# Turning a third of each head's softmax blocks by DMA instead of by TensorE in a fused decoder layer

## The chip, the cores and the metric

The kernel runs on one core of a Trainium2 chip. The metric is the device time of one execution in microseconds (us). Before the change it was 1101.77 us, the median of three runs (1101.6 to 1101.96).

## The reference, cut to what matters

The layer is attention, a residual and a LayerNorm, then a gated block that picks one of four experts by token, then a sparse feed-forward block. The change touches attention alone. There are 4 batches of 512 tokens, width 512, 16 heads of width 32, all in fp32:

```python
scores = jnp.einsum('bthd,bshd->bhts', q, k)
mask = jnp.tril(jnp.ones((T, T), dtype=scores.dtype))
scores = scores * mask                       # masked scores are 0, not minus infinity
attn = jax.nn.softmax(scores / T ** 0.5, axis=-1)
out = jnp.einsum('bhts,bshd->bthd', attn, v).reshape(B, T, H * Dh)
return out @ Wo
```

## The kernel before, in words

**Tiling.** Queries are cut into four rows of 128 (r = 0 to 3). Row r needs the keys of blocks 0 to r, which makes 1 + 2 + 3 + 4 = 10 blocks of 128 by 128 a head; what lies above the diagonal enters through sums. A head's rows are handled as three units (`row_blocks`, line 191): unit 0 is rows 2 and 0 (4 blocks), unit 1 is row 3 (4 blocks), unit 2 is row 1 (2 blocks). A batch has 16 heads, so 48 units, and there are 4 batches.

**One unit.** TensorE multiplies the scores into one of three PSUM banks `S` (`scores`). VectorE masks them and takes the maxima (`maxima`, `negated`). ScalarE takes the exponential into an SBUF tile `probs` (`exps`, signal `s_e`). TensorE turns each block with a transpose against `ident` into one of two PSUM banks `TP` (`transposes`, line 505, signal `s_T`). ScalarE copies the turned bank to fp16 (`hi`, line 697), VectorE subtracts that copy from the bank, which gives the low fp16 half (`lo`, line 870, signal `s_lo`). TensorE multiplies both halves by the values, two matmuls a block (`values`, line 521). Once a head's units are through, ScalarE copies the head out (`copy_out`, line 722), which sets `s_oe`.

**Order.** Each engine has one loop over the units, written out by hand. In iteration u TensorE does the transposes of unit u, the scores of unit u + 3, a piece of a projection (three matmuls over 512 columns, `pieces`), and the values of unit u - 2. ScalarE does the exponential of u, then `hi` of u - 1, then, in some iterations, the upper half of a projection (`split_at`) and the copy of a head. VectorE does the maxima of u + 2, `lo` of u - 1, then the split's lower half. GpSimd adds the parts of a head up. In batches 0 to 2 the projections of the rest of this batch and the first half of the next run beside the heads; in the last batch they end at unit 21. After the last unit of a batch stand the value projection of the next batch, the turn of the heads and the output product (`between`); in the last batch `finish`.

**SyncE.** Each projected group g of 128 columns of q or k goes out to DRAM in two DMAs of 256 KB (`halves_out`) and comes back in another arrangement in four of 256 KB (`stack_in`). SyncE runs through these as their inputs become ready, with the load of the next batch's turned x (1 MB, line 420), the load of x for the residual (1 MB, line 427) and, in the last batch, the context (4 MB) between them. All of them are issued from the one queue of SyncE.

Batches, iterations and units are numbered from 0, as in the code; batch 3 is the last.

Of the kernel before, what the change touches and what calls it, by code (L numbers as in the profile page):

```python
# [45 lines left out]
def attention(nc, w_dram, w_split, stacks, ident, idx_all, x_t, x_raw, s_xraw, x_rows,  # L46
# [17 lines left out]
    AHEAD_S, AHEAD_MAX, AHEAD_HI, AHEAD_LO, AHEAD_V = 3, 2, -1, -1, -2  # L64
    RP = 4
# [3 lines left out]
    with ExitStack() as ctx:  # L69
# [17 lines left out]
        probs = [sb(f"probs{i}", [P, T], F32) for i in range(RP)]  # L87
        pt_hi = [sb(f"pt_hi{i}", [P, T], F16) for i in range(RP)]
# [4 lines left out]
        ot_hl = [[sb(f"ot_{h}{i}", [P, KT, P], F32R) for i in range(2)] for h in ("hi", "lo")]  # L93
# [97 lines left out]
        row_blocks = ((2, 0), (3,), (1,))  # L191
# [3 lines left out]
        def places_of(rows):  # L195

            at = [sum((r + 1) * P for r in rows[:i]) for i in range(len(rows) + 1)]
            return list(zip(rows, at)), at[-1]

# [14 lines left out]
        G_AHEAD = 4  # L214
# [9 lines left out]
        turn_at = {25: 0, 33: 1, 46: 2}  # L224
# [164 lines left out]
        def _(sp):  # L389
# [21 lines left out]
            def stack_up(b, g):  # L411
                halves_out(b, g)
                stack_in(b, g)

            def batch(b, more):
                if more:

                    wait_apart(sp, s_passed_sp, [(s_xl, (b + 1) * KT)])
                    sp.wait_ge(s_z, PRIMED + b * NB)
                    sp.dma_start(x_turned, x_t[b + 1]).then_inc(s_xraw, 16)  # L420
                for g in range(G_AHEAD, 2 * NM):
                    stack_up(b, g)

                sp.wait_ge(s_xl, (b + 1 + more) * KT)
                if not more:
                    sp.wait_ge(s_z, PRIMED + b * NB)
                sp.dma_start(x_res, x_rows[b]).then_inc(s_xres, 16)
                if not more:

                    sp.wait_ge(s_pj, B * 2 * NM)  # L430
                    for e in range(len(context.raw)):
                        context.load(sp, e)
                if more:
                    for g in range(2 * NM, 2 * NM + G_AHEAD):
                        stack_up(b, g)
# [20 lines left out]
            for g in (2, 3):  # L456
                halves_out(0, g)
            for g in (2, 3):
                stack_in(0, g)
# [5 lines left out]
        def _(pe):  # L465
# [18 lines left out]
            def scores(b, u):  # L484
# [5 lines left out]
                if u >= SR:  # L490

                    pe.wait_ge(s_e, b * UPB + u - SR + 1)
# [1700 lines left out]
```

## Time and profile before

| | us |
|---|---|
| median of three runs | 1101.77 |
| the profiled execution | 1103.12 |
| its span, first to last instruction | 1101.4 |
| PE busy | 1040.3 (94%) |
| DVE busy | 738.3 (67%) |
| ACT busy | 486.6 (44%) |
| granted TensorE clock, mean | 0.989 |

PE is TensorE, PEld its weight loads, DVE VectorE, ACT ScalarE, POOL GpSimd, SP or SPq SyncE. The attention part ends at about 428 us of the span; what follows (experts, feed-forward) is TensorE work that the change does not touch. The shares above are means over both parts, so they say little of the loop over the heads. There, a timeline of one engine is the view to read. A line of it has the start in the span, the duration, the engine, the line of the kernel, the operation and its tiles. A record can last longer than the distance to the next one, because instructions overlap; where work is added up below, it is the distance from start to start that counts.

### The profile page before, as it was taken

Reading aid. Unit: us, or ns where it says so; the run is one execution under the profiler, and the core shown is the slowest. Engines: PE = TensorE matmul, PEld = TensorE weight load, DVE = VectorE, ACT = ScalarE, POOL = GpSimd, SP = SyncE. Lnnn points to the kernel's source line nnn. Section 1 sums busy time; section 2 is a strip of 40 time slices with the busy share of each in tenths; the row PEclk is TensorE's granted clock in tenths of the full one; section 3 lists DMA queues with packets and bytes.
Section 4 is the critical chain, followed back from the end, with each engine's and each line's share of the span. In section 5 each row is a group of like instructions: output and inputs, shape, how many; then the busy total and the mean of one; then the engine's idle time right before and its main releaser. Section 6 shows DMA issues by size and latency. Waiting matters only on the chain.

```text
span 1101.4 us, 18098 instructions
## 1 busy us (share of the span) xinstructions
PE 1040.3 (94%) x6022; PEld 840.1 (76%) x6023; DVE 738.3 (67%) x1768; ACT 486.6 (44%) x904; POOL 294.7 (27%) x496
## 2 busy tenths in 40 slices
PE   7889998999999875999999999999999999999995
PEld 6667776777777664788888888888888888888884
DVE  6798699778868886566657546445565545654766
ACT  5688488758857884222324222221232122222125
POOL 2186348545643641223220005100000000000224
PEclk9999999999999997999999999999999999999998
DMA  8877366727743742224532003310020001100112
GB/s 263 229 195 195 87 199 188 193 81 183 204 124 106 184 172 76 68 76 153 191 132 90 1 1 39 39 39 1 1 77 10 28 0 38 38 1 1 39 39 77
DMA packets 55217, 106.19 MB, mean 96 GB/s; under 512 B 6240, under 2 KB 8288, under 8 KB 55136
## 3 DMA queue, kind: packets, MB, share of 16 engines
q1 hardware_dynamic: 50256, 90.99, 29.9%
q0 software_dynamic: 4880, 14.18, 3.4%
q8 instruction: 44, 0.72, 0.3%
q14 instruction: 37, 0.30, 0.1%
HBM read 72.11 MB, written 30.94 MB: 94 GB/s over the span
## 4 chain that ended last, share of the span: by engine, by line
PE 58%; DVE 2%; ACT 1%; DMA 0%; issue 0%; POOLq 0%; POOL 0%; ACTq 0%; DVEq 0%
PE f_bank L42 55%; PE f_bank L1636 1%; PE f_bank L1644 1%; PE f_bank L1706 1%; PE f_bank L1660 0%; DVE beats L1973 0%; DVE h L1998 0%; DMA rows<-sorted_dram 0%; DVE rows_kept L2021 0%; ACT rows_kept L1067 0%; ACT fsg L1843 0%; DVE ln_stats L1039 0%; DVE rows_kept L2032 0%; ACT L1890 0%; POOLq L1410 0%
## 5 line engine op out<-in xcount | busy, mean ns | idle before, releaser
L1809 ACT ACTIVATE fsg<-f_bank 128x512 f32<-128x512 f32 x64 | 38.2, 597 | 299.7 <-PE f_bank L42 290.6
L1959 DVE TENSOR_TENSOR h<-f_bank,fsg 128x512 f32<-128x512 f32 x64 | 44.3, 692 | 181.3 <-PE f_bank L42 177.8
L687 ACT ACTIVATE probs<-bank,nmax 128x384 f32<-128x384 f32 (+3 forms) x256 | 131.7, 549 | 16.1 <-DVE nmax L861 13.2
L505 PE MATMUL bank<-ident,probs 128*128 128x128 f32 x640 | 108.6, 284 | 26.8 <-DVE pt_lo L870 13.3
L845 DVE CUSTOM_DVE_ANT_0 bank<-bank,mask 128x384 f32<-128x384 f32 (+3 forms) x256 | 123.3, 504 | 13.9 <-PE bank L494 12.7
L1072 POOL TENSOR_SCALAR ln_var<-ln_mv 128x1 f32<-128x1 f32 x39 | 9.0, 230 | 453.2 <-DVE ln_mv L1041 451.9
L870 DVE TENSOR_TENSOR pt_lo<-bank,pt_hi 128x512 f16<-128x512 f32 (+1 forms) x192 | 115.1, 599 | 16.9 <-ACT pt_hi L697 16.7
L697 ACT ACTIVATE pt_hi<-bank 128x512 f16<-128x512 f32 (+1 forms) x192 | 104.9, 547 | 28.2 <-PE bank L505 27.5
L42 PE MATMUL bank<-x_hi,w_qk 128*128 128x512 f32 x256 | 101.8, 415 | 6.1 <-DVE x_lo L875 5.8
L42 PE MATMUL f_bank<-wd_hi,hs_hi 128*128 128x512 f32 x256 | 99.9, 390 | 0.8 <-issue 0.8
L42 PE MATMUL f_bank<-wd_hi,hs_lo 128*128 128x512 f32 x256 | 99.8, 390 | 0.0
L42 PE MATMUL f_bank<-wd_lo,hs_hi 128*128 128x512 f32 x256 | 99.6, 389 | 0.0
L505 PEld LDWEIGHTS bank<-ident,probs 128*128 128x128 f32 x640 | 66.7, 140 | 39.0 <-ACT probs L687 23.7
L42 PE MATMUL f_bank<-big_hi,wg_hi 128*128 128x512 f32 x240 | 93.8, 391 | 0.0
L42 PE MATMUL f_bank<-big_lo,wg_hi 128*128 128x512 f32 x240 | 93.6, 390 | 0.0
L42 PE MATMUL f_bank<-big_hi,wu_lo 128*128 128x512 f32 x240 | 93.5, 390 | 0.0
L42 PE MATMUL f_bank<-big_hi,wg_lo 128*128 128x512 f32 x240 | 93.4, 389 | 0.0
L42 PE MATMUL f_bank<-big_hi,wu_hi 128*128 128x512 f32 x240 | 93.4, 389 | 0.0
L42 PE MATMUL f_bank<-big_lo,wu_hi 128*128 128x512 f32 x240 | 93.4, 389 | 0.0
L494 PE MATMUL bank<-big_lo 128*128 128x384 f32 (+3 forms) x256 | 83.0, 370 | 1.8 <-DMA big_lo<-k_lo_dram 1.8
L521 PEld LDWEIGHTS bank<-v,pt_hi 128*128 128x128 f16 x640 | 49.4, 97 | 37.8 <-issue 27.3
L1973 DVE TENSOR_TENSOR beats<-mag 128x512 bf16<-128x512 f32 (+4 forms) x51 | 56.2, 1158 | 30.6 <-ACT mag L1821 30.6
(262 smaller groups left out, 2470.4 us busy)
## 6 DMA issues: line engine op xcount, KB each, us to landing
big_lo<-q_hi_dram SPq DMA_DIRECT2D x32, 256.0 KB
big_lo<-q_lo_dram SPq DMA_DIRECT2D x32, 256.0 KB
big_lo<-k_hi_dram SPq DMA_DIRECT2D x32, 256.0 KB, 3.9
big_lo<-k_lo_dram SPq DMA_DIRECT2D x32, 256.0 KB, 5.2
rows<-sorted_dram SPq DMA_DIRECT2D x19, 256.0 KB, 2.7
q_hi_dram<-q_hi SPq DMA_DIRECT2D x16, 256.0 KB, 3.2
q_lo_dram<-q_lo SPq DMA_DIRECT2D x16, 256.0 KB, 3.1
k_hi_dram<-k_hi SPq DMA_DIRECT2D x16, 256.0 KB, 3.6
```

Source lines behind the costliest of these rows:

```text
L42: ins = pe.matmul(out, a(k, i), b(k, j), start=(n == 0), stop=(n == len(chain) - 1))
L494: ins = pe.matmul(S[u % SR][:, at:at + cols(r)], stack[0][m % 2][:, h, r * P:(r + 1) * P], stack[1][m % 2][:, h, 0:cols(r)], start=True, s ...
L505: ins = pe.transpose(TP[u % TR][:, j * P:(j + 1) * P], probs[u % RP][:, j * P:(j + 1) * P], ident[:, :])
L521: ins = pe.matmul(out[:, at:ONE + 1], p, v3[:, j, c, at:ONE + 1], start=(n == 0), stop=(n == len(chain) - 1))
L687: ins = act.activation(probs[u % RP][:, at:at + cols(r)], S[u % SR][:, at:at + cols(r)], ACT.Exp, bias=nmax[:, r, c:c + 1])
L697: act.activation(pt_hi[u % RP][:, 0:n], TP[u % TR][:, 0:n], ACT.Copy).then_inc(s_hi, 1)
L845: dve.tensor_tensor_reduce(out=S[u % SR][:, at:at + cols(r)], in0=S[u % SR][:, at:at + cols(r)], in1=mask[:, T - cols(r):T], scale=1.0, sc ...
L870: dve.tensor_tensor(pt_lo[u % RP][:, 0:n], TP[u % TR][:, 0:n], pt_hi[u % RP][:, 0:n], ALU.subtract).then_inc(s_lo, 1)
L1636: ins = pe.transpose(XB[q % 2][:, k * P:(k + 1) * P], rows[q][:, k * P:(k + 1) * P], ident[:, :])
L1809: act.activation(fsg[v % 2][:, :], GB[v % 2][:, :], ACT.Silu).then_inc(s_sg, 1)
L1959: dve.tensor_tensor(h[r % 2][:, j, :], UB[v % 2][:, :], fsg[v % 2][:, :], ALU.mult).then_inc(s_h, 1)
L1973: dve.tensor_tensor(beats[:, at:at + w, tw], mag[:, i:i + 1, tw].broadcast_to([P, w, tw.stop - tw.start]), mag[:, i + 1:J, tw], ALU.is_ge) ...
```

## The change

Units become rows 1 and 0 (3 blocks), row 2 (3 blocks), row 3 (4 blocks). The first of them is not turned by TensorE any more. Its exponential is written to the PSUM bank `TP` that its transposes would have filled (bank `S[0]` for unit 0 of a batch), ScalarE and VectorE split it there into the fp16 halves `p_hl` (128 x 768), and SyncE issues one transposing DMA from `p_hl` to `p_turned` (`turn`), six blocks of 128 by 128. There are two such pairs of tiles (`RD`). TensorE's values of that unit come last in its head (`valued`), and all values come three units behind instead of two (`AHEAD_V`). TensorE has no transposes in an iteration whose unit is turned by DMA.

The exponential of such a unit gets a wait on `s_lo` of the unit two before it, since it writes the bank that this one is read from. SyncE goes through the units in order: at each third unit it waits for `s_lo` and issues the turn; the transfers that it issued as they became ready are now tied to units (`in_at`, `out_at`, `X_AT`, `RES_AT`, `CTX_AT`), and the context comes in 16 pieces of 256 KB, one a unit from unit 27. The output halves `ot_hl` are placed over other tiles.

```diff
-    AHEAD_S, AHEAD_MAX, AHEAD_HI, AHEAD_LO, AHEAD_V = 3, 2, -1, -1, -2
-    RP = 4
+    AHEAD_S, AHEAD_MAX, AHEAD_HI, AHEAD_LO, AHEAD_V = 3, 2, -1, -1, -3
+    RP, RD = 4, 2
...
-        row_blocks = ((2, 0), (3,), (1,))
+        row_blocks = ((1, 0), (2,), (3,))
...
+        def by_dma(u):
+
+            return u % UPH == 0
...
+        def valued(slot):
+
+            return slot + 1 if slot % UPH < UPH - 1 else slot - (UPH - 1)
...
+        out_at = {0: 3, 6: 4, 12: 5, 18: 6, 21: 7, 33: 8, 36: 9, 45: 10}
+        in_at = {0: 2, 3: 3, 9: 4, 15: 5, 24: 6, 27: 7, 39: 8, 42: 9}
+        X_AT, RES_AT, CTX_AT = 0, 42, 27
...
+            def turn(b, u):
+
+                d = b * HEADS + u // UPH
+                n = places_of(units[u][2])[1]
+                wait_apart(sp, s_passed_sp, [(s_lo, b * UPB + u + 1)])
+                if d >= RD:
+                    sp.wait_ge(s_pv, b * UPB + slot_of(u) - RD * UPH + 1)
+                sp.dma_start(p_turned[d % RD][:, 0:2 * n // P, :], p_hl[d % RD][:, 0:2 * n],
+                             transpose=True).then_inc(s_pt[d % RD], 16)
...
             def batch(b, more):
+                for u in range(UPB):
+                    if by_dma(u):
+                        turn(b, u)
+                    if u in in_at and due(b, more, in_at[u]):
+                        stack_in(b, in_at[u])
+                    if u in out_at and due(b, more, out_at[u]):
+                        halves_out(b, out_at[u])
+                    if u == X_AT and more:
+
+                        wait_apart(sp, s_passed_sp, [(s_xl, (b + 1) * KT)])
+                        sp.wait_ge(s_z, PRIMED + b * NB)
+                        sp.dma_start(x_turned, x_t[b + 1]).then_inc(s_xraw, 16)
+                    if u == RES_AT:
+
+                        sp.wait_ge(s_xl, (b + 1 + more) * KT)
+                        if not more:
+                            sp.wait_ge(s_z, PRIMED + b * NB)
+                        sp.dma_start(x_res, x_rows[b]).then_inc(s_xres, 16)
+                    if not more and 0 <= u - CTX_AT < KT * len(context.raw):
+
+                        if u == CTX_AT:
+                            sp.wait_ge(s_pj, B * 2 * NM)
+                        context.load(sp, *divmod(u - CTX_AT, KT))
...
-            def values(b, u):
+            def values(b, slot):
+                u = valued(slot)
...
-                pe.wait_ge(s_lo, b * UPB + u + 1)
+                if by_dma(u):
+                    d = b * HEADS + c
+                    pe.wait_ge(s_pt[d % RD], 16 * (d // RD + 1))
+                else:
+                    pe.wait_ge(s_lo, b * UPB + u + 1)
...
-                    if u < UPB:
+                    if u < UPB and not by_dma(u):
                         transposes(b, u)
...
+                if by_dma(u):
+                    to = S[u % SR] if u == 0 else TP[u % TR]
+                    if u > 0:
+
+                        act.wait_ge(s_lo, b * UPB + u - TR + 1)
...
                 n = places_of(units[u][2])[1]
-                act.wait_ge(s_T, b * UPB + u + 1)
...
+                if by_dma(u):
+                    act.wait_ge(s_e, b * UPB + u + 1)
...
-                    if u % UPH == 2 and UPH <= u < UPB:
-                        copy_out(b, u // UPH - 1)
+                    if u % UPH == 0 and u >= 2 * UPH:
+                        copy_out(b, u // UPH - 2)
```

## Rows read from the trace of the kernel before

**Rows 1.** Loops, batches 1-3: PE, PEld, DVE, ACT, POOL busy; clock, DMA share, GB/s.
```profile
138.00:209.00 71.00, 65.17 (x608) 51.02 (x606) 66.03 (x255) 59.84 (x136) 45.87 (x75) 1.00 0.68 194
239.00:310.00 71.00, 65.79 (x611) 51.28 (x610) 61.72 (x224) 60.31 (x137) 42.10 (x71) 1.00 0.70 190
340.00:405.00 65.00, 55.12 (x569) 44.61 (x567) 58.08 (x219) 57.83 (x132) 36.61 (x67) 1.00 0.63 191
```

**Rows 2.** Timeline of PE in batch 1: start, duration, line, output and inputs, count.
```profile
201.16 0.41 PE L505 MATMUL bank<-ident,probs 128*128 128x128 f32 x2
201.33 0.36 PE L494 MATMUL bank<-big_lo 128*128 128x256 f32 x1
201.53 0.40 PE L42 MATMUL bank<-x_hi,w_qk 128*128 128x512 f32 x1
...
202.23 0.22 PE L521 MATMUL bank<-v,pt_hi 128*128 128x97 bf16 x1
...
202.63 0.66 PE L505 MATMUL bank<-ident,probs 128*128 128x128 f32 x4
203.05 0.48 PE L494 MATMUL bank<-big_lo 128*128 128x384 f32 x2
```

**Rows 3.** Timeline of ACT there; in brackets idle time before, and its releaser.
```profile
203.20 0.72 ACT L687 ACTIVATE probs<-bank,nmax 128x512 f32<-128x512 f32 x1
203.77 0.64 ACT L697 ACTIVATE pt_hi<-bank 128x512 f16<-128x512 f32 x1
204.25 0.52 ACT L687 ACTIVATE probs<-bank,nmax 128x256 f32<-128x256 f32 x1
204.67 0.60 ACT L697 ACTIVATE pt_hi<-bank 128x512 f16<-128x512 f32 x1
205.76 0.50 ACT L722 ACTIVATE o_part<-bank 128x388 f32<-128x388 f32 x1 [0.50 <-POOL rsum L247]
206.16 0.83 ACT L687 ACTIVATE probs<-bank,nmax 128x384 f32<-128x384 f32 x2
206.87 0.40 ACT L697 ACTIVATE pt_hi<-bank 128x256 f16<-128x256 f32 x1
207.13 0.71 ACT L687 ACTIVATE probs<-bank,nmax 128x512 f32<-128x512 f32 x1
...
210.07 0.49 ACT L722 ACTIVATE o_part<-bank 128x388 f32<-128x388 f32 x1 [0.27 <-PE bank L521]
```

**Rows 4.** The same in batch 3, past the last projection.
```profile
397.74 0.49 ACT L722 ACTIVATE o_part<-bank 128x388 f32<-128x388 f32 x1
...
401.64 0.49 ACT L722 ACTIVATE o_part<-bank 128x388 f32<-128x388 f32 x1
```

**Rows 5.** DVE line 870: its group at 512 columns, one instruction at 256.
```profile
L870 DVE TENSOR_TENSOR pt_lo<-bank,pt_hi 128x512 f16<-128x512 f32 x128 | 88.0, 687 | 4.9 <-ACT pt_hi L697 4.9
...
207.30 0.42 DVE L870 TENSOR_TENSOR pt_lo<-bank,pt_hi 128x256 f16<-128x256 f32 x1
```

**Rows 6.** Who waited for whom in the loop of batch 1: total, times, longest.
```profile
ACT pt_hi L697 <- PE bank L505: 7.4, 7, 4.0
PEld bank L505 <- ACT probs L687: 4.9, 12, 0.9
```

**Rows 7.** The page's DMA queue of SyncE: packets, MB, share of 16 engines.
```profile
q1 hardware_dynamic: 50256, 90.99, 29.9%
```

**Rows 8.** Landings of the 32 stores of line 397, 256 KB each.
```profile
DMA to landing us min/median/max: 2.0/3.5/5.3
```

**Rows 9.** SyncE's issues in batch 1, then the stretch in which they moved.
```profile
177.08 1.28 SPq L408 DMA_DIRECT2D big_lo<-k_hi_dram  x2
178.41 0.91 SPq L408 DMA_DIRECT2D big_lo<-k_lo_dram  x2
181.05 0.40 SPq L427 DMA_DIRECT2D x_raw<-x  x1
...
178.00:186.00 8.00, 7.26 (x70) 5.74 (x67) 6.74 (x28) 6.82 (x17) 7.11 (x10) 1.00 0.94 262
```

More of the change, by code:

```diff
@@ L87, in attention @@
         probs = [sb(f"probs{i}", [P, T], F32) for i in range(RP)]
+        with ExitStack() as octx:
+            ot_hl = [[octx.enter_context(nc.sbuf_tensor(f"ot_{h}{i}", [P, KT, P], F32R)) for i in range(2)]
+                     for h in ("hi", "lo")]
         pt_hi = [sb(f"pt_hi{i}", [P, T], F16) for i in range(RP)]
@@ L92, in attention @@
         o_tmp = [sb(f"o_tmp{i}", [P, NB - 1, HPT, HD], F32) for i in range(2)]
-        ot_hl = [[sb(f"ot_{h}{i}", [P, KT, P], F32R) for i in range(2)] for h in ("hi", "lo")]
+        p_hl = [sb(f"p_hl{i}", [P, 2 * WIDE * P], F16) for i in range(RD)]
+        p_turned = [sb(f"p_turned{i}", [P, 2 * WIDE, P], F16) for i in range(RD)]
+        s_pt = [sem(f"s_pt{i}") for i in range(RD)]
         mask = sb("mask", [P, T], F32)
@@ L409, in stack_in @@
                                  scratch[side][half].rearrange("(h r) t -> r h t", r=HD)).then_inc(s_st[side], 16)
-            def stack_up(b, g):
-                halves_out(b, g)
-                stack_in(b, g)
-            def batch(b, more):
-                if more:
[L418 to L435, printed above, removed]
+            def turn(b, u):
[6 more added lines that the diff above has]
+                             transpose=True).then_inc(s_pt[d % RD], 16)
@@ new lines, in due @@
+            def due(b, more, g):
+                return (more or g < 2 * NM) and (g >= G_AHEAD or b == 0)
+            def batch(b, more):
+                for u in range(UPB):
[18 more added lines that the diff above has]
+                        context.load(sp, *divmod(u - CTX_AT, KT))
+                if more:
+                    stack_in(b, 2 * NM + G_AHEAD - 2)
+                    halves_out(b, 2 * NM + G_AHEAD - 1)
+                    stack_in(b, 2 * NM + G_AHEAD - 1)
@@ L455, in _ @@
                 sp.dma_start(wo_raw[k], w_dram[3][:, k, :]).then_inc(s_wo_in, 16)
[L456 to L459, printed above, removed]
+            halves_out(0, 2)
             for b in range(B):
@@ L504, in transposes @@
                 for j in range(places_of(rows)[1] // P):
-                    ins = pe.transpose(TP[u % TR][:, j * P:(j + 1) * P], probs[u % RP][:, j * P:(j + 1) * P],
-                                       ident[:, :])
+                    ins = pe.transpose(TP[u % TR][:, j * P:(j + 1) * P],
+                                       probs[turned_index(u) % RP][:, j * P:(j + 1) * P], ident[:, :])
                 ins.then_inc(s_T, 1)
-            def values(b, u):
+            def values(b, slot):
+                u = valued(slot)
                 m, h, rows = units[u]
                 c = m * HPT + h
-                if u % UPH == 0 and c >= OR:
+                if slot % UPH == 0 and c >= OR:
                     pe.wait_ge(s_oe, b * HEADS + c - OR + 1)
-                pe.wait_ge(s_lo, b * UPB + u + 1)
+                if by_dma(u):
[3 more added lines that the diff above has]
+                    pe.wait_ge(s_lo, b * UPB + u + 1)
+                blocks = places_of(rows)[1] // P
                 for r, place in places_of(rows)[0]:
@@ L519, in values @@
                     for n, (j, half, at) in enumerate(chain):
-                        p = (pt_hi, pt_lo)[half][u % RP][:, place + j * P:place + (j + 1) * P]
+                        if by_dma(u):
+                            p = p_turned[d % RD][:, half * blocks + place // P + j, :]
+                        else:
+                            p = (pt_hi, pt_lo)[half][turned_index(u) % RP][:, place + j * P:place + (j + 1) * P]
                         ins = pe.matmul(out[:, at:ONE + 1], p, v3[:, j, c, at:ONE + 1],
@@ L851, in negated @@
                 c = m * HPT + h
-                rs = slice(rows[-1], rows[0] + 1, 2) if len(rows) > 1 else slice(rows[0], rows[0] + 1)
+                rs = slice(rows[-1], rows[0] + 1)
                 dve.wait_ge(s_mx, (b * HEADS + c) * NB + rows_done[u % UPH])
@@ L935, in batch @@
                         negated(b, u + AHEAD_MAX)
+                    if b == 0 and u == 0:
+                        lo(0, 0)
                     if b > 0 and u == LAST_ROW_AT:
```

56 lines of the change are left out of this document (40 added, 16 removed).

## The prediction

> **What bounds the kernel now.** I read the busy times of the loops over the heads first. TensorE is busy 65.2 and 65.8 of 71 us in batches 1 and 2, VectorE 66.0 and 61.7, ScalarE 59.8 and 60.3 [rows 1]. So TensorE leads, with two engines close behind, and it idles some 5 to 6 us a loop. The waits name the partners: ScalarE's copy `hi` waits 7.4 us for the transposes, TensorE's weight loads 4.9 us for the exponentials [rows 6]. The three engines hand each unit round, and each has little to give. The timeline then gives the pace. A head with projections takes 210.07 - 205.76 = 4.31 us from one head copy to the next [rows 3]. Past the last projection, in batch 3, it takes 401.64 - 397.74 = 3.90 us [rows 4]. TensorE has far less to do there, so 3.90 us is the pace of the ring ScalarE, VectorE, TensorE and not of any one engine. Outside the loops nothing is edited; what comes after attention starts later or earlier with it, one to one.
>
> **What TensorE is given.** Three transposes of ten leave each head. Two blocks take 201.33 - 201.16 = 0.17 us to the next matmul, four take 203.05 - 202.63 = 0.42 us [rows 2]. Before, a head has 0.42 + 0.42 + 0.17 = 1.01 us of them; after, one group of four and one of three, 0.42 + 0.29 = 0.71 us. That is 0.30 us a head, 4.8 us a batch, 19 us in all if TensorE set the pace everywhere. It does so at most in batches 0 to 2, where 14.4 us is the most it can bring.
>
> **What ScalarE is given.** Its instructions keep their columns: exponentials of 128, 256, 384 and 512, and `hi` of 384, 384, 512 for 512, 512, 256. From start to start a head costs 0.71 (384 and 128) + 0.26 (`hi` 256) + 0.57 (512) + 0.48 (`hi` 512) + 0.42 (256) + 0.48 + 0.40 (head copy) = 3.32 us [rows 3]. New is a wait. The exponential of unit 3k writes the bank out of which VectorE reads `lo` of unit 3k - 2, and ScalarE's own instruction just ahead of it is the `hi` that this `lo` needs. So ScalarE must stand still over a full `lo` once a head. A `lo` of 384 columns lies between the 0.42 us at 256 and 0.687 at 512 [rows 5], so 0.56 us. It starts 0.03 us after the record of `hi` ends (207.30 against 206.87 + 0.40) [rows 3, 5]; the record ends 0.12 us after the next instruction could have started (0.60 against 0.48), and I allow 0.1 us back: 0.82 us a head. Nothing fills it, since the split and the head copy stand in iterations 3k, behind the exponential. Queued behind it on ScalarE are `hi` of 3k - 1 and the head copy; TensorE's scores of 3k + 3 wait for this exponential. ScalarE's round is then 3.32 + 0.82 = 4.14 us, and with the splits, the x copies and the like, (59.8 - 16 x 3.32) / 16 = 0.42 us a head [rows 1], 4.56 us or 73 us a batch. The loop takes 71 to 72 us today. So TensorE's gain runs into this wait. If ScalarE can use all its idle time under it, the loop stays as it is; I take 1 us more for each of batches 0 to 2, **3 us**, with bounds of -9.6 (two thirds of TensorE's 14.4) and +10. In batch 3, past the projections, 4.14 replaces 3.90 us: some 9 heads by 0.24 us, **2.2 us** (0 to 4). The price of an exponential into PSUM has no row; it reads PSUM either way, and I take it as equal, within 0.05 us either side (x 64 = 3 us). VectorE keeps its columns too.
>
> **What the transposing DMA costs.** It moves 128 x 768 x 2 = 196,608 bytes. The trace has no transposing transfer. The queue's 50,256 packets took 29.9% of 16 x 1101.4 us, 105 ns a packet, 17.3 GB/s an engine [rows 7]. By bytes the turn occupies the engines for 196,608 / 16 / 17.3 = 0.71 us; if it goes as 768 runs of 256 bytes at the mean price of a packet, 768 / 16 x 0.105 = 5.0 us. I take the lower end, since the queue's packets are of 2 KB on average and a short one should cost less. A 256 KB store lands 2.0 us after issue at best [rows 8], so about 1 us beyond its transfer; I take 0.7 + 1.0 us and 0.4 us for the issue.
>
> The Trainium skill has two prices. VectorE: DVE Perf Modes, section The three transpose paths, gives 1309 ns for one 128 x 128 block in 2 bytes; six would be an estimated 7.9 us. DMA: Bandwidth & Descriptors, section Latency and other measured facts, gives 261 GB/s, by which the turn is an estimated 0.75 us. No run so far shows either; the first would bring the last rival below.
>
> **Who waits for it.** A loop's mean head is 71 / 16 = 4.4 us. In the loop the turn is due four units after its `lo`, 4 x 4.4 / 3 = 5.9 us. Alone it lands in about 2.1 us, behind one `stack_in` (1 MB) in some 4 to 5 us. Both are covered. It is not covered where more lies in the queue. At unit 42 of batches 0 to 2 SyncE issues the turn, then `stack_in` of group 9 and the residual's x, 2 MB. The trace has that pair: issues at 177.08 to 181.05, and 8.0 us from 178 to 186 at 0.94 of the engines [rows 9]. The queue is in order, so the turn of unit 45, issued one head (4.4 us) later, starts after 1.2 + 0.7 + 8.0 = 9.9 us and lands at 9.9 + 0.7 + 1.0 = 11.6, that is 7.2 us after its issue. What TensorE has left until the last values of the batch is short: the four transposes of unit 47 (0.4), one projection piece of the next batch (0.7: 202.23 - 201.53 [rows 2]), four groups of values at 0.3 and the handing round of unit 47, some 2.8 us. TensorE stands for 4.4 us, three times: **13.2 us** (0 to 24). Nothing hides it, because all of TensorE's next work, the value projection, is behind these matmuls in its order. In batch 3 the residual's x and a context piece, 1.25 MB, lie ahead: 1.2 + 0.7 + 5.0 + 1.7 - 4.0 = 4.6 us after issue against 2.3 us of work left, **2.3 us**. At unit 0 of batch 0 `stack_in` of group 2, two stores and the x load make 2.5 MB, 10 us; the turn of unit 3 lands 8.5 us after its issue against 5.9: **2 us** (0 to 4). The next `lo`s are not behind SyncE, but each later issue of its queue is.
>
> **The sum.** 3 + 2.2 + 13.2 + 2.3 + 2 = 22.7 us. On the profiled execution's 1103.1 us that is 1125.8; it stood 1.3 us above the median, so 1124 us.
>
> **The rivals.**
> - *TensorE's relief comes through* (faster). ScalarE has over 10 us of idle time a loop [rows 1] and could put the new wait into it, and the turns could land in time, if the queue at unit 42 is empty when the 2 MB start. Then two thirds of 14.4 us are kept: 1101.8 - 9.6 = 1092 us. Against it: ScalarE's idle time is 11 us a loop, the new wait 16 x 0.82 = 13.
> - *The DMA engines become the bound* (slower by far). At 5.0 us a turn, 80 us a batch come on top of 0.69 x 71 = 49 in the loop [rows 1], 129 us against 71; some 20 us of this fit between the loops, if the turns could run ahead, which two buffers forbid. Each head then takes at least 5.0 plus its share of the other traffic, 3.1: (8.1 - 4.4) x 64 = 237 us, 1339 us. It decides from about 1.3 us a turn on, where 3.1 + 1.3 reaches 4.4. By the skill's 1309 ns a block (the page named above) it would be an estimated 11 us a head, above 1500 us.
> - *Nothing changes.* The waits at the batch ends are 3 us in all and the loops give them back: 1102 us.
>
> **How the numbers follow.** The forecast, 1105 to 1145 us, gets 0.50; the relief 0.27; no change 0.06; the DMA bound 0.17. A measurement of this kernel can tell about 0.2%, 2.2 us, from no change. Slower is 0.67, same 0.06, faster 0.27. The range has to hold 8 in 10: from 1090, which takes in nearly all of the relief, to 1165, which takes in the forecast's upper bounds and turns of up to about 2 us.
>
> **What would show it.** On ScalarE, idle time of about 0.8 us before the exponential of each third unit, released by `lo` of VectorE, in nearly all heads; before, ScalarE hardly waited for `lo` at all. On TensorE, a wait of 4 to 5 us for `p_turned` ahead of the last values of batches 0, 1 and 2, and none in mid-batch. TensorE's busy time in a loop down by about 5 us with the loop no shorter. The prediction is wrong if the head period in mid-batch falls to 4.1 us, if TensorE waits for `p_turned` at every head, or if the turn of unit 45 lands within 3 us of its issue.

## The result, and the profile after

The changed kernel took 1183.49 us (median of 4, 1177.97 to 1186.74) against 1101.87 us for the kernel before on the same chip: a ratio of 1.073 [1.071, 1.075], **81 us slower**. The direction was forecast, the size was not: 1124 us was predicted, and 1165 us was the upper end.

The page of the changed kernel (busy time of the engines; then the granted clock in 40 slices; then the packets and the main DMA queue):

```profile
PE 1046.1 (89%) x5830; PEld 840.8 (71%) x5831; DVE 744.5 (63%) x1768; ACT 483.6 (41%) x904; POOL 295.0 (25%) x496
...
PEclk9998899989988998989999999999999999999998
...
DMA packets 106609, 118.78 MB, mean 101 GB/s; under 512 B 57632, under 2 KB 59680, under 8 KB 106528
...
q1 hardware_dynamic: 101648, 103.58, 36.7%
```

The engines have about as much to do as before: VectorE's and ScalarE's busy times move by 6 and 3 us. TensorE's busy time even rose by 6 us though it has 448 transposes instead of 640; the granted clock of the attention part is lower, at 8 and 9 tenths in most of its slices above. The queue has twice the packets that it had [rows 7].

One stretch holds the attention part in each kernel, from 36 us to the first transposes behind it. First the kernel before, then the changed one (columns as in [rows 1]: length, PE, PEld, DVE, ACT, POOL busy, clock, DMA share, GB/s):

```profile
36.00:430.90 394.90, 354.29 (x2939) 277.27 (x2937) 327.07 (x1113) 291.52 (x634) 203.87 (x353) 0.99 0.59 163
```

```profile
36.00:505.70 469.70, 360.89 (x2745) 278.85 (x2744) 332.12 (x1111) 287.53 (x632) 204.35 (x353) 0.91 0.72 163
```

The whole difference of the two spans, 1176.2 - 1101.4 = 74.8 us, lies here: 469.7 - 394.9. It is TensorE's idle time, 40.6 us before and 108.8 after (+68.2), and its busy time (+6.6). What TensorE waited for, with total, count and longest, in the changed kernel:

```profile
PE bank L550 <- ACT probs L749: 26.2, 36, 1.7
PE bank L539 <- DMA big_lo<-k_lo_dram: 19.7, 6, 4.5
PE bank L575 <- DMA p_turned<-p_hl: 18.7, 4, 6.5
...
PE bank L539 <- ACT bank L749: 8.7, 12, 1.2
PE bank L601 <- DVE v_tail L967: 7.5, 3, 2.5
PE bank L539 <- ACT probs L749: 6.7, 2, 4.0
PE bank L575 <- DVE pt_lo L945: 3.4, 4, 1.0
PE bank L539 <- issue: 2.8, 1, 2.8
PE bank L550 <- DVE p_hl L945: 1.3, 4, 0.4
```

and in the kernel before, whose L505 is the later L550 and whose L547 is L601:

```profile
PE bank L505 <- DVE pt_lo L870: 13.3, 21, 1.5
...
PE bank L505 <- ACT probs L687: 9.8, 21, 0.7
PE bank L547 <- DVE v_tail L892: 1.6, 3, 0.5
...
PE bank L521 <- DVE pt_lo L870: 0.7, 1, 0.7
```

L539 are the scores. Nine of their waits, the rows with `k_lo_dram`, `probs` and "issue", are of 1.9 to 4.5 us and stand ahead of the first scores of a new group of four heads. There the code waits for the stacks of q and k (`s_st`), so I count all nine to them, whatever name the trace gives: 19.7 + 6.7 + 2.8 = 29.2 us. (This is a reading of the code and of the places; the trace names a stack for six of the nine. The waits for stacks in the other runs are counted in the same way.) With 18.7 us for the turns, 8.7 for ScalarE's late exponentials at the scores, 7.5 - 1.6 = 5.9 for `v_tail`, and 30.9 - 23.8 = 7.1 for the rest of the handing round, that makes 69.6 us, about the 68.2 us of added idle time. **The stacks are the largest item, and the prediction has none for them.**

The distance between the copies of two heads (`o_part` on ScalarE) shows where. Worked out from the starts of these copies, batch 2, us:

| copy to copy | 4-5 | 5-6 | 6-7 | 9-10 | 11-12 | 12-13 | 14-15 | to the next batch |
|---|---|---|---|---|---|---|---|---|
| kernel before | 4.84 | 4.25 | 4.38 | 5.21 | 4.37 | 4.40 | 1.95 | 34.3 |
| changed | 5.30 | 5.86 | 5.24 | 7.70 | 4.70 | 4.53 | 8.77 | 40.3 |

The wait for the last turn lies in 14-15, that for a stack in 5-6 and 9-10.

### The profile page after: what moved, and what is told of

It is laid out like the page before. It is cut to its first block, busy times and chain, and to the rows that moved or that the text cites. A ratio compares the mean times of both kernels' runs of the same rounds, so it can differ in the third digit from the quotient of the medians.

```text
span 1176.2 us, 17788 instructions
## 1 busy us (share of the span) xinstructions
PE 1046.1 (89%) x5830; PEld 840.8 (71%) x5831; DVE 744.5 (63%) x1768; ACT 483.6 (41%) x904; POOL 295.0 (25%) x496
## 3 DMA queue, kind: packets, MB, share of 16 engines
q1 hardware_dynamic: 101648, 103.58, 36.7%
## 4 chain that ended last, share of the span: by engine, by line
PE 56%; DMA 0%; DVE 0%; issue 0%; ACT 0%; POOLq 0%; POOL 0%; ACTq 0%; DVEq 0%
PE f_bank L42 53%; PE f_bank L1714 1%; PE f_bank L1722 1%; PE f_bank L1784 1%; PE f_bank L1738 0%; DMA rows<-sorted_dram 0%; POOLq L1488 0%; POOL out L1660 0%; ACT rows_kept L1145 0%; ACTq L1488 0%; DVE ln_stats L1117 0%; DVE rows_kept L2110 0%; DVE gt_lo L1981 0%; ACT gt_hi L1865 0%; DVE ln_mv L1119 0%
## 5 line engine op out<-in xcount | busy, mean ns | idle before, releaser
L918 DVE CUSTOM_DVE_ANT_0 bank<-bank,mask 128x256 f32<-128x256 f32 (+3 forms) x256 | 123.3, 504 | 41.1 <-PE bank L539 37.8
L539 PE MATMUL bank<-big_lo 128*128 128x256 f32 (+3 forms) x256 | 87.7, 389 | 39.7 <-DMA big_lo<-k_lo_dram 21.3
L550 PE MATMUL bank<-ident,probs 128*128 128x128 f32 x448 | 80.0, 298 | 29.9 <-ACT probs L749 26.2
L945 DVE TENSOR_TENSOR pt_lo<-bank,pt_hi 128x384 f16<-128x384 f32 (+1 forms) x128 | 79.6, 622 | 19.1 <-ACT pt_hi L768 18.4
L749 ACT ACTIVATE probs<-bank,nmax 128x384 f32<-128x384 f32 (+1 forms) x128 | 83.7, 657 | 0.7 <-DVE nmax L937 0.7
L768 ACT ACTIVATE pt_hi<-bank 128x384 f16<-128x384 f32 (+1 forms) x128 | 71.5, 559 | 20.3 <-PE bank L550 20.3
L539 PEld LDWEIGHTS bank<-big_lo 128*128 128x128 f32 x256 | 46.3, 203 | 45.3 <-issue 32.7
L550 PEld LDWEIGHTS bank<-ident,probs 128*128 128x128 f32 x448 | 50.2, 149 | 38.6 <-ACT probs L749 34.0
```

What stands on the lines that cost most here:

```text
L539: ins = pe.matmul(S[u % SR][:, at:at + cols(r)], stack[0][m % 2][:, h, r * P:(r + 1) * P], stack[1][m % 2][:, h, 0:cols(r)], start=True, s ...
L550: ins = pe.transpose(TP[u % TR][:, j * P:(j + 1) * P], probs[turned_index(u) % RP][:, j * P:(j + 1) * P], ident[:, :])
L749: ins = act.activation(to[:, at:at + cols(r)], S[u % SR][:, at:at + cols(r)], ACT.Exp, bias=nmax[:, r, c:c + 1])
L768: act.activation(to[:, 0:n], (S[0] if u == 0 else TP[u % TR])[:, 0:n], ACT.Copy).then_inc(s_hi, 1)
L918: dve.tensor_tensor_reduce(out=S[u % SR][:, at:at + cols(r)], in0=S[u % SR][:, at:at + cols(r)], in1=mask[:, T - cols(r):T], scale=1.0, sc ...
L945: dve.tensor_tensor(out, (S[0] if u == 0 else TP[u % TR])[:, 0:n], high[:, 0:n], ALU.subtract).then_inc(s_lo, 1)
```

## The experiments

Each is an edit of the changed kernel; of the longer edits only the lines that matter are shown, and "..." stands for the rest. The lines that the trace gives shift a little between kernels: the scores are L539 here, L532, L541 or L540 there.

### One block a turn (small_turn)

```diff
-                sp.dma_start(p_turned[d % RD][:, 0:2 * n // P, :], p_hl[d % RD][:, 0:2 * n],
+                sp.dma_start(p_turned[d % RD][:, 0:1, :], p_hl[d % RD][:, 0:P],
...
```

> The transposing DMA moves one block of 128 by 128 instead of six (so the value products of rows 0 and 1 use zeros or stale halves and the output is not the layer's); every wait and every issue stays in place. The changed kernel has a span of 1176 us. If the traffic of the turns is what delays all else (1.6 us of all sixteen engines a turn by the page, 64 turns), the waits for p_turned and for the stacks shrink and the time falls by 25 us or more, to 1150 us or less. If it is the order in which SyncE issues, tied to the units, the turns' size matters little: 1165 to 1180 us. If it is ScalarE's wait for lo, nothing changes: within 5 us of the changed kernel.

Measured 1.0631 [1.0608, 1.0653], 1171.75 us: with five sixths of the turns' bytes gone, 1.0 point of 7.3 came back (a point is one per cent of the time of the kernel before). That is in the range expected where the order matters and the size little. The bytes are not nothing, though: TensorE's waits for turns fell from 18.7 to 13.1 us and those for stacks from 29.2 to 23.4. The turn on SyncE's queue, in the changed kernel and here (duration of the issue, min/median/max in ns):

```profile
L446 SPq DMA_TRANSPOSE p_turned<-p_hl x64: 1210/1216/1847, 34.2 to 478.4; - x64
```

```profile
L450 SPq DMA_TRANSPOSE p_turned<-p_hl x64: 1093/1096/1433, 34.7 to 466.2; - x64
```

```profile
q1 hardware_dynamic: 60688, 93.10, 30.7%
```

The issue of one block costs SyncE 1.10 us, of six 1.21 us. The difference of the queue's shares in the two kernels gives an estimate of the traffic: (36.7% x 1176.2 - 30.7% x 1164.6) x 16 = 1186 us of one engine for 40,960 packets of 256 bytes, 29 ns each. Six blocks, 768 packets, are 1.39 us of all 16 engines.

### The residual's x earlier, the stacks earlier, both (res_early, stacks_early, res_stacks)

```diff
-        X_AT, RES_AT, CTX_AT = 0, 42, 27
+        X_AT, RES_AT, CTX_AT = 0, 30, 27
```

> The 1 MB load of the residual's x is issued at unit 30 instead of unit 42. By the theory that the last turn of a batch is late because stack_in of group 9 and this load lie ahead of it, the waits for p_turned at the ends of batches 0 to 2 (5.4 to 6.5 us each on TensorE) fall to 2 to 3 us and the stretch at half clock behind them shortens: 10 to 15 us less than the changed kernel. It may give 3 us back in each batch at the scores of unit 36, whose stack is loaded just before. If the turn itself is slow whatever lies ahead, no more than 3 us change.

```diff
-        out_at = {0: 3, 6: 4, 12: 5, 18: 6, 21: 7, 33: 8, 36: 9, 45: 10}
-        in_at = {0: 2, 3: 3, 9: 4, 15: 5, 24: 6, 27: 7, 39: 8, 42: 9}
+        out_at = {0: 3, 6: 4, 10: 5, 15: 6, 21: 7, 31: 8, 36: 9, 42: 10}
+        in_at = {0: 2, 3: 3, 9: 4, 12: 5, 21: 6, 24: 7, 33: 8, 39: 9}
```

> The loads of the stacks of groups 5 to 9 and the stores of groups 5, 6, 8 and 10 are issued 2 to 6 units earlier in SyncE's order, nothing else changes. TensorE of the changed kernel waits nine times for a stack at its scores, 1.9 to 4.5 us each, 29 us in sum. If this is SyncE's order and not the sum of the traffic, most of it goes: 15 to 30 us less than the changed kernel. If the DMA engines are simply full, the waits move elsewhere and less than 5 us is gained. The last turn of a batch should also land earlier, since group 9's load no longer stands right before it: its wait falls by up to 3 us.

Both edits together:

> The changed kernel with both edits of SyncE's order, the residual's load at unit 30 and the stacks earlier, alone 1.0605 and 1.0527 against 1.0733. If they act on separate waits, 1.040 or less (13 and 23 us less). If the second already takes what the first gives, 1.045 to 1.053. all1, which has three more edits, is 1.0445: the difference to it is what those three bring together.

Measured 1.0605 [1.0570, 1.0639], 1.0527 [1.0495, 1.0559], and for both 1.0451 [1.0433, 1.0468]. No instruction is added or removed, only the order in SyncE's queue changes, and with both edits 31 of 81 us come back. The two alone gave 1.3 and 2.1 points, both together 2.8, so they act on waits that are mostly separate. TensorE's waits with the residual's x early, then with the stacks early:

```profile
PE bank L539 <- DMA big_lo<-k_lo_dram: 26.5, 8, 4.8
...
PE bank L575 <- DMA p_turned<-p_hl: 9.6, 5, 2.6
```

```profile
PE bank L575 <- DMA p_turned<-p_hl: 32.3, 16, 3.7
```

With x out of the way of the last turn, the wait for turns halves (18.7 to 9.6 us), and the stacks stay at 29.6. With the stacks early, one wait for them of 1.0 us is left, and waits for turns come in their place, 16 instead of 4. Whatever is put ahead in the one queue, the other is late.

### VectorE's `lo` of the next batch after the sums (lo_after)

```diff
                         negated(b + 1, AHEAD_S - 1)
-                        lo(b + 1, 0)
                     elif step == "sum":
                         v_above(b + 1, r)
+                if more:
+                    lo(b + 1, 0)
```

> VectorE computes lo of a batch's unit 0 after the sums of v instead of before them. In the changed kernel TensorE waits 2.5 us for v_tail once in each of batches 1 to 3 (0.5 us before the change), and the clock is at its lower level for some us after it. By that theory this gives back 2 us three times and some of the slow stretch, 6 to 10 us in sum. If the wait for v_tail comes from elsewhere (ScalarE's hi of that unit, ahead of it on ScalarE), less than 2 us.

Measured 1.0687 [1.0659, 1.0715], half a point under the changed kernel, whose interval it just touches. The wait for `v_tail` fell from 7.5 to 1.5 us, what it was in the kernel before (1.6), and a wait of the first scores for `p_hl` (4.0 us in three) came in.

### No wait of ScalarE for `lo` (sbuf_exp)

The exponential of a unit that is turned by DMA goes to an SBUF tile of its own, from which `hi` and `lo` are made:

```diff
-                    to = S[u % SR] if u == 0 else TP[u % TR]
-                    if u > 0:
-
-                        act.wait_ge(s_lo, b * UPB + u - TR + 1)
+                    to = e_sb[(b * HEADS + u // UPH) % RD]
+                    if b * HEADS + u // UPH >= RD:
+
+                        act.wait_ge(s_lo, b * UPB + u - RD * UPH + 1)
...
```

> The exponential of the units that DMA turns goes to a tile in SBUF of its own instead of the PSUM bank, so that ScalarE need not wait for lo of two units before; TensorE's scores of unit 3 wait for the exponential again. ScalarE of the changed kernel idles 1.1 us before 63 of these exponentials, 70 us in sum. By the theory that this wait makes the heads longer, the idle time goes and a head without other trouble takes 4.1 instead of 4.4 us: 10 to 20 us less than the changed kernel. If the heads are bound by the transfers and by VectorE, less than 5 us. The lo of these units reads two SBUF tiles; should that be slower than from PSUM, VectorE loses some of it.

Measured 1.0733 [1.0715, 1.0752], no change at all, where 10 to 20 us less were expected if the wait counted. ScalarE's waits in the changed kernel, then here:

```profile
ACT bank L749 <- DVE nmax L934: 67.0, 62, 2.5
ACT o_part L793 <- PE bank L575: 25.9, 8, 8.2
```

```profile
ACT pt_hi L766 <- PE bank L548: 42.2, 38, 5.6
ACT o_part L791 <- PE bank L573: 39.8, 27, 8.1
...
ACT e_sb L747 <- DVE nmax L932: 16.7, 13, 2.5
```

The first row is the wait that the prediction describes, 62 times 1.08 us (`nmax` is named since VectorE makes it right behind that `lo`). Here it shrinks to 16.7 us, and ScalarE waits for TensorE instead, 42.2 us for the transposes. TensorE's own waits here:

```profile
PE bank L573 <- DMA p_turned<-p_hl: 23.6, 6, 6.5
PE bank L537 <- issue: 20.2, 5, 4.8
...
PE bank L537 <- DMA big_lo<-k_lo_dram: 11.6, 3, 4.5
```

With a further wait of 3.6 us for a stack, which the trace puts down to `probs`, turns and stacks make 59.0 us, against 18.7 + 29.2 = 47.9 us in the changed kernel. In batch 2 the intervals 6-7 to 8-9 became shorter, 5.24 to 4.42 for the first, and those with a stack longer: 5.86 and 7.70 us turned into 6.56 and 10.17. A head that runs faster only arrives earlier at a transfer that is late.

### Value products over the last turn's wait (cover)

```diff
+                    if more and u + AHEAD_V == UPB - 2:
+
+                        v_product(0, steps=range(1))
                     if more and u + AHEAD_V == UPB - 1:
-
-                        v_product(0, steps=range(1))
+                        v_product(0, steps=range(1, KT))
+                        v_product(1)
...
```

> At the end of batches 0 to 2 TensorE does the value projection of the next batch's blocks 0 and 1 ahead of the last values instead of behind them, some 5 us of work while the last turn is on its way. The wait for p_turned falls from 5.4 to 6.5 us to under 2 us and no half-clock stretch follows: 15 to 20 us less than the changed kernel if nothing else is late next. The turn of the heads then has no such cover any more, which can give 1 to 3 us a batch back, in which case 6 to 14 us.

Measured 1.0723 [1.0682, 1.0763], so nothing came back that can be told from noise, against all that was expected (6 us at the least). The wait for turns fell from 18.7 to 9.1 us, and TensorE's turn of the heads, which hangs on the last head copy, now waited 9.7 us (3 times, up to 3.2) for `o_raw`. The stacks stayed at about what they were, 30.7 us against 29.2.

### All of these edits, and all with one block a turn (all1, all1_small)

> The five edits together: residual's load at unit 30, stacks earlier, lo of unit 0 behind the sums, exponential to SBUF, value projection ahead of the last values. If the costs are separate, the gains add up: 12 + 22 + 4 + 12 + 12, some 60 us, and the time is 1115 to 1130 us. If TensorE's relief then comes through, it is at or below 1105 us. If they are all one and the same cost (too much in one queue), the sum is far less: above 1145 us.

> all1 with turns of one block of six (the value products of rows 0 and 1 use zeros or stale halves, so the output is not the layer's). all1 is 1.0445 of the kernel before, and its TensorE still waits 20 times for p_turned, 33 us in sum. If the bytes of the turns are what is left, most of these waits go and the ratio is 1.02 or less. If the place of a turn in the queue behind the bulk transfers is what is left, the ratio stays at 1.035 or more.

Measured 1.0445 [1.0418, 1.0472] and 1.0343 [1.0311, 1.0375]. The first is no better than the two queue edits alone (1.0451), so the other three together bring nothing even where the queue is eased. The wait for `o_raw` (9.7 us) that `cover` brings in is there too, so a gain from one of the three may be hidden by it. The gains did not add up (1115 to 1130 us): 1150.1 us is the case "one and the same cost". One block instead of six is again worth 1.0 point.

### The changed order without the DMA turns (pe_turns, pe_turns_early)

All ten blocks are turned by TensorE again. Kept are the new order of the rows, the values three units behind, and SyncE's transfers tied to units:

```diff
         def by_dma(u):
...
-            return u % UPH == 0
+            return False
...
```

> The changed kernel with its unit order, its values three units behind and SyncE's order with its waits for lo at each third unit, but all ten blocks turned by TensorE again and no transposing DMA, so also without ScalarE's wait for lo. If the tying of SyncE's bulk transfers to the units costs by itself, TensorE still waits about nine times for a stack at its scores, 25 to 30 us in sum, and the time is 20 to 40 us over the kernel before. If it is the turns that cost (their traffic, their late landing, ScalarE's wait), the time is within 8 us of the kernel before.

> pe_turns with the residual's load at unit 30 and the stacks issued earlier. pe_turns has 12 us of waits ahead of its scores that the kernel before does not have. If they are SyncE's order alone, they go and the ratio is 0.998 to 1.003. If the order of the rows or the values three units behind cost, it stays above 1.005.

Measured 1.0081 [1.0063, 1.0099], and with the residual's x and the stacks early 1.0066 [1.0049, 1.0083]. The order costs 9 us, and where the stacks stand hardly matters as long as no turns stand between them: the two intervals overlap. So most of the 9 us come from the order of the rows or from the values three units behind, which no run tells apart. TensorE's waits for stacks are 9.6 us in the first (7 times, up to 4.5).

### The same, with 64 turns that nobody waits for (idle_turns)

As the kernel above, but SyncE issues the 64 transposing DMAs from a constant tile, at the places of the changed kernel:

```diff
-                sp.dma_start(p_turned[d % RD][:, 0:2 * n // P, :], p_hl[d % RD][:, 0:2 * n],
+                sp.dma_start(p_turned[d % RD][:, 0:2 * n // P, :], p_hl[0][:, 0:2 * n],
...
```

> As pe_turns (TensorE turns all ten blocks, SyncE's order tied to the units), but SyncE issues the 64 transposing DMAs as well, from a constant tile to tiles that no engine reads. Nobody waits for them. pe_turns was 1.0081 of the kernel before, the changed kernel 1.0733. If what costs is that these DMAs delay the bulk transfers (1.2 us of issue, 1.4 us of the DMA engines each), TensorE's waits for stacks grow as in the changed kernel and the ratio is 1.04 or more. If it is that TensorE, ScalarE and VectorE depend on them, the ratio stays under 1.02.

Measured 1.0372 [1.0344, 1.0400], a little under the 1.04 expected and far over 1.02. **DMAs that no engine waits for cost 2.9 points.** Between heads, batch 2, from the copies' starts:

| copy to copy | 4-5 | 5-6 | 6-7 | 8-9 | 9-10 | 11-12 | 14-15 |
|---|---|---|---|---|---|---|---|
| no turns | 4.44 | 4.27 | 4.38 | 4.45 | 5.41 | 4.42 | 0.92 |
| idle turns | 4.44 | 5.98 | 4.38 | 4.45 | 10.91 | 4.44 | 0.90 |

All other heads agree to 0.08 us. In the four batches the copies 2, 6 and 10, those behind a new group's scores, take 34.6 us more in sum, the whole difference of the spans (1143.8 - 1109.1 = 34.7). TensorE's waits ahead of these scores make 26.1 us of it: they are 35.7 us here (9 times, up to 7.5) and 9.6 without turns. The trace of one such place: without turns, SyncE's issues of a stack of k, and the scores that need it,

```profile
286.04 0.78 SPq L436 DMA_DIRECT2D big_lo<-k_hi_dram  x2
286.87 1.25 SPq L436 DMA_DIRECT2D big_lo<-k_lo_dram  x2
...
293.42 0.42 PE L532 MATMUL bank<-big_lo 128*128 128x256 f32 x2 [0.28 <-issue]
```

and with idle turns:

```profile
308.13 1.21 SPq L449 DMA_TRANSPOSE p_turned<-p_hl  x1
309.46 0.98 SPq L437 DMA_DIRECT2D big_lo<-k_hi_dram  x2
310.49 0.91 SPq L437 DMA_DIRECT2D big_lo<-k_lo_dram  x2
...
319.56 0.66 PE L541 MATMUL bank<-big_lo 128*128 128x256 f32 x2 [4.26 <-issue]
```

The last head copy ahead of the scores is at 292.82 and at 314.97. So the first issue comes 6.8 us ahead of it without turns and 5.5 with them, 1.3 us later, about one turn's issue. From the last issue's end to the scores it takes 293.42 - 288.12 = 5.3 us and 319.56 - 311.40 = 8.2, 2.9 us more. Together 4.2 us, and the stall grew by 4.0. The larger part is thus not the later issue: the turn issued at 308.13 landed 5.5 us later, at 313.6, so its transfer was still under way when the stack was issued behind it. After the stall the same two matmuls last 0.66 instead of 0.42 us, and the granted clock in the slice from 320 to 321 us is 0.50; the whole interval 9-10 grew by 5.5 us.

### The idle turns with the stacks early (idle_rs)

> The idle turns (all blocks turned by TensorE, 64 transposing DMAs that nobody waits for) with the residual's x and the stacks earlier. idle_turns measured 1.0372, pe_turns_early 1.0066. If the turns' price is only that stacks arrive late behind them, issuing the stacks earlier takes most of it away: 1.015 or less. If the turns' traffic slows the others whatever the order, it stays: 1.03 or more.

Measured 1.0202 [1.0185, 1.0219]. Against 1.0372 the earlier stacks take 1.7 of 2.9 points away; 1.4 points stay above the same kernel without turns (1.0066). It is neither of the two expected ends: over half of the price goes with another order, the rest stays at this order.

### The last turn of each batch by TensorE (last_pe, last_pe_rs)

Unit 45 gets its transposes back; the other 15 heads of a batch keep their DMA:

```diff
         def by_dma(u):
...
-            return u % UPH == 0
+            return u % UPH == 0 and u < UPB - UPH
...
```

> The unit 45 of each batch (last head, rows 1 and 0) is turned by TensorE again and has no DMA; the 15 other heads of a batch keep theirs. If the late last turn is what the batch ends cost, the three stalls before the last values (6.2, 5.4 and 6.5 us) go, with v_tail's wait (3 x 2.5) and the slow clock after them (batch end 40.5 instead of 34.2 us): some 3 x (6.0 + 6.3) = 37 us less less 3 x 2 us for the transposes, so about 1152 us, 1.045. If the stall only hides transfers that are late anyway, the next batch starts later on its stacks and less than 10 us comes back: 1174 us or more, 1.065.

> The same with the residual's x at unit 30 and the stacks one place earlier (res_stacks measured 1.0451). If batch-end stall and stack waits are separate costs, they add: about 1.0451 - 0.02 = 1.025 (1129 us). If the earlier stacks have already taken the batch-end stall away, 1.040 or more.

Measured 1.0413 [1.0396, 1.0431], 1148.64 us, and with the residual's x and the stacks early 1.0435 [1.0417, 1.0452]. **Four of 64 turns carry 35 of the 81 us**, as expected (1152). One part of that expectation failed: `v_tail`'s 7.5 us stayed. TensorE's waits with the last turn removed, then with the stacks early too:

```profile
PE bank L540 <- DMA big_lo<-k_lo_dram: 28.1, 8, 4.2
PE bank L551 <- ACT probs L750: 24.2, 34, 1.2
```

```profile
PE bank L551 <- ACT probs L750: 26.8, 38, 1.2
PE bank L576 <- DMA p_turned<-p_hl: 22.2, 13, 3.2
```

The first has no wait for a turn left, and the stacks' waits stay (28.1 us in this row, 30.8 with the one named "issue"). The second trades them for 22.2 us of turns. My expectation that the two gains add (1.025) fell. The queue edits alone give 1.045, the last turn on TensorE alone 1.041, both 1.044.

## Why the prediction was right in direction and wrong in size

Four kernels divide the 7.3 points, each closer to the changed kernel than the one before it. The third column is the start of the last head copy, from the traces:

| | ratio | last copy, us |
|---|---|---|
| kernel before | 1 | 407.9 |
| the new order alone | 1.0081 | 414.8 |
| and 64 turns that nobody waits for | 1.0372 | 449.5 |
| 60 real turns, none for a batch's last head | 1.0413 | 454.7 |
| the changed kernel | 1.0733 | 482.5 |

So 0.8 points are order, 2.9 the turns' place in the queue and their traffic, 3.2 the last turn of each batch. The 0.4 between the third and the fourth is a net of several things (with real turns TensorE and ScalarE wait for turns and for `lo`, TensorE has fewer transposes, four turns are gone), and the intervals of the two runs touch. The shares also hold for this sequence alone: `last_pe_rs` shows that gains do not add.

**What bounds the kernel now.** The reading of the three engines, each with little to give, was right for the kernel before. It left out the fourth resource. The DMA share stands in the same rows, 0.68 to 0.70 [rows 1], and I used it in a rival only.

**TensorE's relief** (0.30 us a head, at most 14.4 us). The transposes went, 2939 - 2745 = 194 instructions, and the loop did not shorten. The four intervals 10-11 to 13-14 of batch 2, which hold no late transfer, make 17.46 us in the changed kernel, 17.49 before, and 17.04 where TensorE has all blocks back in the new order. Without ScalarE's new wait (`sbuf_exp`) they make 17.12, so even then the fewer transposes bring nothing. The rival of the relief (chance 0.27) is refuted.

**ScalarE's new wait** (0.82 us a head, 3 + 2.2 us on the time). It came nearly as described, 62 times at 1.08 us, and was worth nothing in the total: without it the time is the same. The inference from a wait that is there to a time that it costs failed, and with it 5.2 us of the sum. Without the wait, heads that need no stack got up to 0.8 us shorter, and TensorE then stood that much longer at the turns and the stacks (59.0 against 47.9 us).

**The price of a turn** (0.4 us issue, 0.71 us of the engines, landing after 2.1). All three were too low: 1.21 us, about 1.39 us, and on the changed kernel's queue

```profile
DMA to landing us min/median/max: 2.7/3.4/9.9
```

The engine price was read from 105 ns a packet and a mean rate [rows 7]. By `small_turn` the turn's short packets cost 29 ns, 8.8 GB/s an engine instead of 17.3. It lies far nearer to the lower bound than to 5.0 us, as was chosen, but is twice the lower bound. The issue had no row of its own kind; it makes 64 x 1.21 = 77 us of the one queue. The Trainium skill's 1309 ns a block (VectorE: DVE Perf Modes, The three transpose paths) would make an estimated 7.9 us for six. Six together took 1.39 us of the engines and landed a median of 3.4 us after issue, so here the blocks of one transfer did not come one after another at that price. The Trainium skill's 261 GB/s (DMA: Bandwidth & Descriptors, Latency and other measured facts) would make an estimated 0.75 us; this case has 196,608 bytes in 1.39 us, 141 GB/s.

**"Both are covered"** in mid-batch. This is the step that failed. I asked only whether the turn itself would be in time, and in the changed order it is: in mid-batch TensorE never waits for one. What the turn does to the stacks queued behind it got one clause ("each later issue of its queue is") and no term in the sum. The stacks were in time before, TensorE waited 1.8 us for them in all. In the new order without turns it waits 9.6 us for them. With 1.2 us of issue and 1.4 us of traffic a head in the same queue they are late nine times by 1.9 to 4.5 us, 29.2 us in the changed kernel; idle turns bring the 9.6 us to 35.7 and the time up by 34.6. The rival "the DMA engines become the bound" put its turning point at 1.3 us a turn, and the measured 1.39 is just past it. It named the right resource and the wrong form: with idle turns no head that needs no new stack got longer. How much of the lateness is issue and how much traffic is not settled; at the place shown above 1.3 us are later issue and 2.9 us come after it.

**The batch end** (4.4 us three times, 13.2). The mechanism was right, in its place and its parts. The queue and TensorE there:

```profile
355.71 1.21 SPq L446 DMA_TRANSPOSE p_turned<-p_hl  x1
357.04 0.98 SPq L436 DMA_DIRECT2D big_lo<-k_hi_dram  x2
358.07 2.13 SPq L436 DMA_DIRECT2D big_lo<-k_lo_dram  x2
360.25 0.43 SPq L471 DMA_DIRECT2D x_raw<-x  x1
360.80 1.85 SPq L446 DMA_TRANSPOSE p_turned<-p_hl  x1
```

```profile
363.37 0.40 PE L42 MATMUL bank<-big_hi,x_lo 128*128 128x512 f32 x1
370.25 0.59 PE L575 MATMUL bank<-v,p_turned 128*128 128x97 bf16 x6 [6.48 <-DMA p_turned<-p_hl]
...
371.65 0.63 PE L42 MATMUL bank<-big_hi,x_lo 128*128 128x512 f32 x1
```

From the start of the turn's issue TensorE has 3.0 us of work left (2.8 forecast), and the values start 9.5 us after it (the turn lands after 9.4; 7.2 forecast). The stalls are 6.2, 5.4 and 6.5 us. They are 18.1 of the 27.8 us that the last turn costs by the table's last column (35 us by the medians; the profiled execution of the changed kernel, 1177.97 us, was its shortest). The other 9.7 us had no step in the prediction. By the head copies of the two kernels, 4.2 lie in the same three intervals, 5.2 between the last copy and the next batch's first, 1.5 at the end of batch 3, and the rest of the attention part is 1.2 shorter. One cause that the trace shows there is the **clock** behind the stall. The same stretch in windows (columns as above; the DMA share is rough in windows this short):

```profile
362.00:366.00 4.00, 1.25 (x11) 0.77 (x11) 1.74 (x4) 0.71 (x3) 1.40 (x3) 1.00 1.07 205
366.00:370.00 4.00, 0.00 (x0) 0.00 (x0) 0.00 (x0) 0.00 (x0) 0.00 (x0) 0.54 1.13 317
370.00:371.00 1.00, 0.75 (x7) 0.75 (x8) 0.00 (x0) 0.12 (x1) 0.00 (x0) 0.50 0.86 330
371.00:372.00 1.00, 1.00 (x3) 0.79 (x3) 0.52 (x3) 0.37 (x1) 0.00 (x0) 0.50 0.00 0
372.00:373.00 1.00, 1.00 (x4) 0.72 (x3) 0.90 (x4) 0.00 (x0) 0.00 (x0) 0.50 0.53 80
373.00:374.00 1.00, 1.00 (x6) 0.82 (x5) 0.88 (x2) 0.00 (x0) 0.00 (x0) 0.91 1.11 307
```

While TensorE stands the clock falls to 0.50, the 1.2 GHz level, and the first 3 us of the next work run at it, a matmul of 512 columns in 0.63 instead of 0.40 us. At the two earlier batch ends the work behind the stall runs at it for some 3 and 6 us. Half of these 12 us, about 6 us, is an estimate of what the clock costs there.

**The other small terms.** The 2 us at the start of batch 0 (8.5 - 5.9 is 2.6 us, in fact) are not a turn that somebody waits for: the head 1-2 of that batch is 7.69 us against 5.16, but 10.52 where TensorE has all blocks, and TensorE waits there for a stack. The end of batch 3 (2.3 us) came out smaller: TensorE waited 0.5 us for the turn, and the last head copy comes 1.5 us later behind the one before it than with that turn by TensorE. Nothing was foreseen of the value projection's wait for `v_tail` (5.9 us more), whose removal alone gave half a point, barely clear of the noise.

**Of the marks named in advance,** two were met: the idle time of ScalarE in nearly all heads, and the wait of 4 to 5 us (in fact 5.4 to 6.5) ahead of the last values. The third was half met: the loop is no shorter, but TensorE's busy time did not fall, it rose by 6.6 us over the attention part at the lower clock. "None in mid-batch" held for `p_turned`, but no mark had been named for `big_lo`, where the time went.

**What stays open.** How much of the time the clock itself costs beyond that estimate: the attention part has 81 slices of 1 us below 0.75 of the clock against 8 before (16 with the order alone, 55 with idle turns, 62 with the last turn by TensorE), but no run holds the clock while the stalls stay. And what part of the turns' price in the loop is issue and what part traffic, the 1.4 points that idle turns keep with the stacks early included. A second issuing queue for the turns wasn't tried; it might tell the two apart.

## What to carry to other kernels

Before a small transfer that is needed soon is put on a queue that also carries megabytes, price both directions: how late it comes behind the large ones, and how late the large ones come behind it, issue time included. A wait that certainly appears has a price only if nothing else ends later; take it away in thought, and ask what the engine would wait for then. The last transfer of a stage is another case than the same transfer in its middle, since the work that covered it has run out: in this kernel that one was better left on TensorE.

## What the runs showed of the hardware

- The issue of a transposing DMA from SBUF to SBUF holds SyncE's queue for 1.10 us with one block of 128 x 128 in fp16 and 1.21 us with six. A plain issue of 256 KB takes 0.4 to 0.6 us in most of these rows. So the time of the issue hardly depends on the number of blocks.
- Its packets are of 256 bytes at 29 ns of one engine each, worked out from the queue's shares with six blocks and with one. That is 8.8 GB/s, half the mean rate of this queue in the kernel before (17.3).
- In a TensorE stall of 6.5 us the granted clock went from 1.00 to 0.50 before the stall was over, and 3 us after work began again it stood at 0.91.
- A turn that is issued 0.1 us behind a stack and 1 MB of x lands 9.4 us after its issue, where the median of the 64 is 3.4.
